# Moving the weight setup of a fused graph layer into the layer's own engine programs

## The reference

```python
x = x + gnn(layernorm(x), adj, wq, bq, wk, bk, wv, bv, wo, bo, w1, b1, w2, b2, alpha1, gamma1, alpha2, gamma2)
x = x + ffn(layernorm(x), gamma_in, slots1, gamma2, w_slot2, f_w1, f_b1, f_w2, f_b2)

def gnn(x, bias, ...):                      # 8 heads of 48 columns
    q, k, v = split_heads(x @ wq + bq), split_heads(x @ wk + bk), split_heads(x @ wv + bv)
    attn = softmax(q @ k.T * 48 ** -0.5 + bias)
    x = rmsnorm(x + (attn @ v) @ wo + bo, alpha1, gamma1)
    return rmsnorm(x + silu(x @ w1 + b1) @ w2 + b2, alpha2, gamma2)   # 384 -> 1536 -> 384
```

## Time and profile before

| | us |
|---|---|
| median of 3 runs | 3043.75 (3042.86 to 3047.78) |
| the profiled execution's own time | 3044.84 |
| its span in the profile | 3043.1 |
| mean granted TensorE clock | 0.979 of full |

### The profile page before, as it was taken

How to read it: one execution, slowest core, us unless ns; L and a number is a source line. 1 busy time by engine, 2 the same in 40 slices (tenths; PEclk the granted TensorE clock), 3 DMA queues, 4 the chain that set the end, 5 groups by cost and what they waited for, 6 DMA issues and landing times. The chain is left out here.

```text
span 3043.1 us, 63201 instructions
## 1 busy us (share of the span) xinstructions
PE 2847.6 (94%) x21971; PEld 2745.6 (90%) x21971; DVE 1898.3 (62%) x3029; ACT 1511.9 (50%) x3986; POOL 1476.6 (49%) x1486
## 2 busy tenths in 40 slices
PE   2899999999999999999999857999899999999996
PEld 2899999999999999999999846998899999999993
DVE  3466666666666666666666624765677777777764
ACT  3455454545555554545555424675455555544440
POOL 0344435354444434344444514553577777777760
PEclk9899999999999999999999968999999999999999
DMA  3010101011010101001010114552766666666799
GB/s 131 13 42 26 47 26 47 24 36 36 26 47 26 47 26 47 24 31 41 26 47 26 36 46 136 153 146 64 232 208 206 207 206 206 208 209 209 247 319 337
DMA packets 276739, 320.70 MB, mean 105 GB/s; under 512 B 17304, under 2 KB 275608, under 8 KB 276504
## 3 DMA queue, kind: packets, MB, share of 16 engines
q1 hardware_dynamic: 267960, 307.17, 32.4%
q10 hardware_dynamic: 8704, 12.58, 1.1%
HBM read 260.97 MB, written 58.72 MB: 105 GB/s over the span
## 5 line engine op out<-in xcount | busy, mean ns | idle before, releaser
L1567 PE MATMUL u_bank<-x_in,x_w 128*128 128x256 f32 x4608 | 574.1, 283 | 5.7 <-DVE x_w L1661 5.7
L1567 PEld LDWEIGHTS u_bank<-x_in,x_w 128*128 128x128 f32 x4608 | 569.2, 192 | 5.8 <-issue 5.8
L949 POOL TENSOR_TENSOR hT_lo<-h_tmp,hT_hi 128x512 fp32r<-128x512 f32 x192 | 247.1, 1287 | 454.0 <-DVE hT_hi L838 452.8
L1730 POOL TENSOR_TENSOR x_aT<-x_act,x_aT 128x512 fp32r<-128x512 f32 x128 | 299.4, 2339 | 181.2 <-ACT x_aT L1638 181.2
L411 PE MATMUL m_bank<-yT_hi,w_hi 128*128 128x256 f32 x1152 | 341.6, 296 | 1.5 <-ACT h_tmp L683 1.5
L1629 ACT ACTIVATE x_gelu<-u_bank,x_b1T 128x256 f32<-128x256 f32 x256 | 121.9, 476 | 408.6 <-PE u_bank L1567 408.6
L1726 POOL TENSOR_TENSOR x_w<-expert_raw,x_w 128x768 fp32r<-128x768 f32 x128 | 274.1, 2142 | 103.5 <-DVE x_w L1669 103.5
L411 PE MATMUL m_bank<-yT_hi,w_lo 128*128 128x256 f32 x1152 | 323.7, 281 | 0.0
L411 PE MATMUL m_bank<-yT_lo,w_hi 128*128 128x256 f32 x1152 | 323.5, 281 | 0.0
L683 ACT ACTIVATE h_tmp<-m_bank,b1c 128x256 f32<-128x256 f32 x384 | 157.2, 471 | 273.3 <-PE m_bank L411 273.0
L1579 PE MATMUL o_bank<-x_w,x_aT 128*128 128x384 f32 x1536 | 287.8, 335 | 1.8 <-POOL x_aT L1730 1.8
(11 more groups left out here) (216 smaller groups left out, 6936.4 us busy)
## 6 DMA issues: line engine op xcount, KB each, us to landing
expert_raw<-in_L_ffn_w_dram SPq DMA_DIRECT2D x384, 384.0 KB, 4.7
ws_raw<-in_L_ffn_w_slot_dram SPq DMA_DIRECT2D x32, 576.0 KB, 6.8
x_in<-in_x_dram SPq DMA_DIRECT2D x32, 384.0 KB, 3.3
x_res<-in_x_dram SPq DMA_DIRECT2D x32, 384.0 KB
residual<-f_sb SPq DMA_DIRECT2D x32, 384.0 KB, 2.5
yn<-yn_sb SPq DMA_DIRECT2D x32, 384.0 KB, 2.5
expert_out<-x_o SPq DMA_DIRECT2D x64, 192.0 KB, 3.0
slots2T<-residual SPq DMA_DIRECT2D x8, 1536.0 KB, 12.2
```

The source lines that it names most:

```text
L949: nc.gpsimd.tensor_tensor(hT[i % 3][1][:], h_tmp[i % 2][:], hT[i % 3][0][:].bitcast(F32), ALU.subtract).then_inc(hl.sem, 1)
L1567: mm = pe.matmul(u_bank[n % BANKS][:, g, :], w1s[i % 2][a][:, c, g, c2 * P:(c2 + 1) * P], xT[e % 2][b][:, c, :], start=c == 0 and j == 0, ...
L1730: nc.gpsimd.tensor_tensor(aTs[i % 2][1][:], aT[i % 2][:], aTs[i % 2][0][:].bitcast(F32), ALU.subtract).then_inc(al.sem, 1)
```

## The change

The setup block and its `free_semaphores()` go. What it did becomes part of the layer's programs, in the first two bodies, under `first(n)`, `first(a)` and `first(m)`, which are true for group 0 only; the loop's code is as before. The staging tiles now share SBUF with those layer tiles that are first written later (`s_sb`, `pT`, `yb`, `h_tmp`, `hT`, `f_sb`, `x_res` and others), so ACT waits for all of its hi copies before the first exponentials, and SP for w2's lo half before it loads `x_res`. The lo halves of w1 and w2, in three pieces each, are POOL's instead of DVE's. The 16 column DMAs of bq are issued by ACT.

```diff
@@ SP
                     sp.dma_start(x_in[:], x_rows[bass.ds(n * GN, GN), :].rearrange("(t p) d -> p t d", p=P)
                                  ).then_inc(x_landed.sem, 16)
+                    if first(n):
+                        for i in (WV, WQ, WK):
+                            load_weight(sp, i)
+                        sp.dma_start(rows["bv"][:], bv.partition_broadcast(P)).then_inc(bv_landed.sem, 16)
+                        sp.dma_start(phi[:], f_slots1.rearrange("k s d -> (k s) d")).then_inc(phi_landed.sem, 16)
+                        load_head_bias(sp, 1, bk)
...
                     sp.dma_start(adj_sb[:], adj[bass.ds(a * GT, GT)].rearrange("t q k -> q t k")
                                  ).then_inc(adj_landed.sem, 16)
+                    if first(a):
+                        load_weight(sp, WO)
+                        for name, src in (("bo", bo), ("alpha1", alpha1), ("gamma1", gamma1)):
+                            sp.dma_start(rows[name][:], src.partition_broadcast(P)).then_inc(rows_landed.sem, 16)
+                        load_weight(sp, W1)
+                        load_weight(sp, W2)
...
                 if m is not None:
+                    if first(m):
+                        sp.wait_ge(w_lo[W2].sem, len(w_copies[W2]))
@@ PE
+            def weight_ready(i):
+                pe.wait_ge(w_lo[i].sem, len(w_copies[i]))
...
+            def phi_transposed():
+                pe.wait_ge(phi_ok.sem, 4)
+                for c in range(DC):
+                    mm = pe.transpose(m_bank[0][:].rearrange("p a b -> p (a b)")[:, tok(c)], phi[:, tok(c)], ident[:])
+                mm.then_inc(phi_T.sem, 1)
...
                 if A: project(a, U_K, wk_s, 1)
+                if first(a): phi_transposed()
                 if M: down(m, 0)
                 if A: scores(a, 0, r); scores(a, 1, r)
@@ ACT
+            def weight_hi(i):
+                act.wait_ge(staged[i].sem, 16)
+                for src, hi, _ in w_copies[i]:
+                    nc.scalar.copy(hi, src).then_inc(w_hi[i].sem, 1)
...
+                if first(n): load_head_bias(act, 0, bq); weight_hi(WV)
+                if first(m): act.wait_ge(rest_landed.sem, 16 * N_REST)
                 if M: silu(m, 0)
                 if A: query(a, 0); query(a, 1)
...
+                if first(a): weight_hi(WO); weight_hi(W1); phi_transposed(); weight_hi(W2); act.wait_ge(consts.sem, 5)
                 if A: nc.scalar.activation(warm[:, 0:1], nhalf[:, 0:1], ACT.Exp)
                 if A: exps(a, 0, 0); exps(a, 0, 1); exps(a, 1, 0); prob_T(a, 0)
...
                 if N: hi_zT(n, 1)
+                if first(n): weight_hi(WQ); weight_hi(WK); phi_squares()
@@ DVE
+                if first(a): dve.wait_ge(bv_landed.sem, 16)
                 if A: values(a, 0); values(a, 1)
...
                 if A: key(a, 1)
+                if first(a): weight_lo(WO)
...
+                if first(n): head_masks()
                 if N: norm_stats(n, x_landed, 16, x_in, st, mv, stats, meanvar)
+                if first(n): weight_lo(WV)
                 if A: context(a, 0); recips(a, 1)
...
                 if N: lo_zT(n, 1)
+                if first(n): weight_lo(WQ); weight_lo(WK); head_biases(); phi_scaled()
...
+                if first(a): rows_scaled()
@@ POOL
+            def weight_lo(i):
+                for n, (src, hi, lo) in enumerate(w_copies[i]):
+                    pool.wait_ge(w_hi[i].sem, n + 1)
+                    nc.gpsimd.tensor_tensor(lo, src, hi.bitcast(F32), ALU.subtract).then_inc(w_lo[i].sem, 1)
...
+                if first(a): weight_lo(W1)
                 if N: power(n, 2, meanvar, mv[:, :, 1], eps_ln, rstd[:, 0, :], rstd[:, 1, :], ve, rstd_ok, 1)
+                if first(n): phi_power()
+                if first(a): weight_lo(W2); pool.wait_ge(rows_landed.sem, 16 * N_ROWS)
                 if M: h_lo(m, 2); h_lo(m, 3)
                 if A:
                     r_bias(a, 0)
```

More of the change, by code:

```diff
@@ L326, in setup_and_layer, with first, load_weight, load_head_bias @@
     S = lambda name, n: sem(ctx, name, n)
+    WQ, WK, WV, WO, W1, W2 = range(6)
+    weights, w_copies = (wq, wk, wv, wo, w1, w2), []
+    for i, parts in enumerate((wq_s, wk_s, wv_s, wo_s, w1_s, w2_s)):
+        if i < 2:
+            w_copies.append(by_head_parts(stage[i], parts))
+        elif i < 4:
+            w_copies.append([[t[:].rearrange("p c f -> p (c f)") if n else t[:] for n, t in enumerate((stage[i], *parts))]])
+        else:
+            views = [stage[i][:].rearrange("p (c f) -> p c f", c=(DC, FC)[i == W2]), *parts]
+            w_copies.append([[v[:, :, 512 * n:512 * n + 512] if i == W1 else v[:, 4 * n:4 * n + 4, :] for v in views]
+                             for n in range(3)])
+    staged, w_hi, w_lo = ([S(f"{name}{i}", 1) for i in range(6)] for name in ("staged", "w_hi", "w_lo"))
+    phi_landed, bv_landed, qk_landed, rows_landed, rest_landed = (S(n + "_landed", 16) for n in (
+        "phi", "bv", "bqk", "rows", "rest"))
+    N_QK, N_ROWS, N_REST = 4 * H, 3, 5 + FC
+    masks_ok, bias_ok, rows_ok = S("masks_ok", 6), S("bias_ok", 2), S("rows_ok", 2)
+    consts, phi_ok, phi_T = S("consts", 5), S("phi", 5), S("phi_T", 1)
+    def first(g):
+        return isinstance(g, int) and g == 0
+    def load_weight(eng, i):
+        w = weights[i]
+        eng.dma_start(stage[i][:].rearrange("p (c f) -> p c f", c=w.shape[0] // P), w.rearrange("(c p) f -> p c f", p=P)
+                      ).then_inc(staged[i].sem, 16)
+    def load_head_bias(eng, n, b):
+        column = b.rearrange("(h e o) -> h e o", e=DH, o=1)
+        for h in range(H):
+            m, g = divmod(h, 4)
+            eng.dma_start(bqk[HG * g:HG * g + HG, n, m:m + 1], column[h, 0:HG]).then_inc(qk_landed.sem, 16)
+            last = HG * g + (DH - HG) * m
+            eng.dma_start(bqk[last:last + DH - HG, n, 2:3], column[h, HG:DH]).then_inc(qk_landed.sem, 16)
     x_landed, adj_landed = S("x_landed", 16), S("adj_landed", 16)
@@ L428, in project @@
                     pe.wait_ge(held.sem, held.at(g, k))
+                if first(g) and n == 0:
+                    weight_ready(WQ if w is wq_s else WK)
                 bank = A_BANK[uses[n]]
@@ L440, in values @@
                         pe.wait_ge(yl.sem, yl.at(g - 1, 2))
+                    if first(g):
+                        weight_ready(WV)
                 bank = A_BANK[U_V[t]]
@@ L495, in project_out @@
                 pe.wait_ge(held.sem, held.at(g, k))
+                if first(g) and t == 0:
+                    weight_ready(WO)
                 bank = A_BANK[U_WO[t]]
@@ L512, in up @@
                 pe.wait_ge(yl.sem, yl.at(g, 2))
+                if first(g) and i == 0:
+                    weight_ready(W1)
+                    pe.wait_ge(phi_ok.sem, 5)
                 if i >= 2:
@@ L527, in down @@
                 pe.wait_ge(hl.sem, hl.at(g, i + 1))
+                if first(g) and i == 0:
+                    weight_ready(W2)
                 for t in range(GT):
@@ L634, in query @@
             def query(g, half):
+                if first(g) and half == 0:
+                    act.wait_ge(bias_ok.sem, 2)
                 act.wait_ge(a_full.sem, a_full.at(g, U_Q[half] + 1))
@@ L962, in body @@
                 if R: power(r, 2, mv2_ok, mv2[:, :, 1], eps_ln, rstd2[:, 0, :], rstd2[:, 1, :], ve2, rstd2_ok, 1)
+                if first(m): pool.wait_ge(rest_landed.sem, 16 * N_REST)
                 if M:
```

188 lines of the change are left out of this document (75 added, 113 removed).

## The result

The changed kernel takes **3014.57 us** (median of 4 runs, 3011.57 to 3015.6). The four runs of the kernel before have a median of 3044.45 us. The ratio is 0.9904, with a 95% interval of 0.9892 to 0.9917: 29.9 us faster at the median, where 34.0 were forecast. The profiled execution took 3015.42 us.

A forecast was written before the change was run, and what follows sets the result against it. PE is busy 94% of the span, so the gain must come from the start, where it works 0.87 of 48 us. -39.3 + 5.0 + 0.3 = -34.0 takes the median from 3043.75 to 3009.7 us, range 3003 to 3019.

The forecast's parts named there:

- part 3: Group 0's softmax: exponentials wait on ACT behind w2's load and copies, starting at 36.5; 5.0 us of the gain lost.
- The common mark: Start of group 1's values, 97.63 us before, 63.6 forecast; what it moves is the gain.
- My bound of 2 us for the time behind the mark: Group 1's values to the end: a difference over 2 us from before would make the whole forecast wrong.
- Part 1: Group 0's rows and wv at the start: z starts at 12.0 instead of 51.29, 39.3 us earlier.
- Part 2: wq, wk, biases and phi on DVE, phi's transposes and wo's subtract hide behind other work; costs nothing.
- Part 4: POOL's w1 and w2 subtracts, 3.5 us a piece, delay group 0's r_bias: 0.3 us lost, all slack used up.
- The clock: PE's clock, low after idling before the first probability transposes: could cost or gain 2 us; zero taken.
- A: Rival on the start: w2 lands earlier or its copies hide, all 39.3 us stay, 3004.4; 7%.
- B: Rival on SP's queue: bv, phi or bk issues stall, w1 and w2 land 7.8 us later, 3017.6; 13%.
- C: Rival on POOL: subtracts at the contended 6.5 us a piece delay r_bias, gain only 19.0, 3024.8; 12%.
- D: Rival on POOL's subtracts: pieces so slow, 9.7 us or beyond, that the gain is gone; slower kernel; 3%.

The follow-up runs named there:

- e2: Changed kernel with bq's 16 column DMAs issued by SP behind bk's instead of by ACT; 3016.13 us (one run).
- e1: Changed kernel with w2's hi copies and POOL's w2 subtracts moved behind group 0's attention; 3007.01 us, ratio to before 0.9874.
- e5: Changed kernel with the loads of rows bo, alpha1 and gamma1 issued behind w1 instead of ahead of it; 3015.05 us (one run).
- e3: Changed kernel with POOL forming the first piece of w2's lo half twice; 3015.92 us (one run).
- e4: Changed kernel with w2's lo half formed by DVE, ahead of the reciprocals, instead of POOL; 3013.43 us (one run).
- e8: Changed kernel with DVE's wait for the rows moved from right before group 0's y_scale to ahead of the reciprocals; 3018.86 us.
- e12: The changed kernel unaltered, run once more on the same chip; 3013.53 us (5 runs), ratio to before 0.9904.
- e7: Changed kernel with 12 larger bq/bk column DMAs, all on SP; wo, w1, w2 loaded before the second x_in; w2's halves after group 0's attention; 3008.88 us.
- e6: Changed kernel with wo, w1 and w2 issued right behind the bk columns, ahead of the second x_in; 3007.76 us, ratio to before 0.9878.
- e10: e7 with bq's columns back on ACT and group 0's adjacency loaded ahead of wo and w1; 3005.85 us, ratio to before 0.9873.
- e11: Changed kernel with 12 larger bq/bk column DMAs (six on ACT, six on SP) and w2's halves after group 0's attention; 3003.44 us, ratio to before 0.9867.

## Why the prediction was right, and where it was not

The prediction was right in sign and mechanism, and 3014.57 lies in the range of 3003 to 3019. It was 4.9 us too low: the start gained 0.7 less than forecast, the exponentials lost 4.5 more behind it (part 3), and the rest, with the stretch behind the mark, nearly cancels.

**The common mark** held: group 1's values moved by 28.7 and the span by 29.5. My bound of 2 us for the time behind the mark was met in that profile (0.8), but is too tight in general: the repeat of the same kernel was 5.1 below before.

**Part 1 (-39.3)**: -38.6. An ACT issue beside SP's cost 0.51 us (0.75 to 8.94 for 16), not 0.46. The nearest row was of the right columns, but of a single queue issuing; the first eleven issues took 0.53 each, the last five 0.47. Statistics, power, copy and subtract came as the rows said (1.02, 0.71, 1.15, 1.36).

**Part 2 (0)**: right. DVE was free of phi at 19.9 and PE met no wait for it; the scores and the wo subtract ended long before the exponentials. e2 shows that this stretch is cover: z 4.8 us earlier brought no gain.

**Part 3 (5.0 lost) is the step that was mis-sized: 9.5 were lost.** The mechanism is as put: ACT's order sets the exponentials behind w2's copies (41.66 and 41.67), and e1, which takes w2 out of that order, gives 7.5 us back. The size had two errors. First, w1: I took bytes at the rate of two 2304 KB loads. From the second `x_in` to w1's copy it took 16.0 us, not 12.9. In the window of 14 to 22 us, where adj, wo and the rows go, the DMA engines moved 224 GB/s at a share of 0.78. The kernel before, from 4 to 24 us, while large loads run:

```profile
4.00:24.00 20.00, 0.00 (x0) 0.00 (x0) 10.35 (x9) 11.39 (x10) 0.00 (x0) 1.00 1.05 388
```

388 GB/s at full share. e5 agrees in direction: 2.0 to 3.4 us for 576 KB of rows that by bytes take 1.4. The rate may not be all: over the 16.02 us the engines moved 302 GB/s, 4.8 MB, 0.8 MB more than the 3968 KB (4.06 MB) I counted, where before it was 0.3 MB more than 4608 KB. If the extra 0.5 MB are bytes of later loads that went in beside w1, they are an estimated 1.2 of the 3.1 us, by 388 GB/s; whose bytes they are I did not settle. Second, w2: its copy began 7.83 after w1's, where I had their landings 6.3 apart; ACT's own copies and phi end at 34.2, so all of it is waiting. With the 0.7 of part 1 that makes 0.7 + 3.1 + 1.5 = 5.3 of w2's delay against the forecast.

How much of this is the kernel and how much this one execution? In five profiles with this order of loads and w2 still ahead of the exponentials (the first, e3, e4, e8, e12) w2's copy began 21.3 to 23.9 us after the second `x_in` was issued, where I had 19.2. So at least 2.1 us were mis-sized in every one, and up to 2.5 more come and go by themselves; the first profile is the latest of the five.

**Part 4 (0.3 lost)**: right in mechanism, 0.1 in size. The pieces took 3.42 us against 3.5, from a line through two sizes; `r_bias` started 0.2 us after y was written, where it was 0.1 before. The estimate of 3.4 by the page GPSIMD Engine Reference of the Trainium skill (section Elementwise — side-by-side cycle accounting) agrees with 3.42. e3 shows that there was no slack, though in e12 there was (2.3 us, as y came late). Missed: half a us between `r_bias` and `y_scale`, which e4 and e8 lose again, for a cause not settled.

**The clock (0, ±2)**: 0 in the first profile (15.88 us from exponentials to `r_bias`, 15.99 before), 2.4 in e12 (18.35). The point value is one of two cases; the other lies just outside my bound. That the first profile met the value is luck, not my reasoning: I had PE idle for 7.7 us, and it idled for 13.2.

**Rivals.** A fell: ACT waited for w2. B fell here: SP's queue passed phi and bk without a stall (0.42 to 0.57 each) and stood still only behind w2, for 9.19 us, in front of rows that nobody wanted yet; e7 shows what it costs when somebody does. C fell here (3.42 a piece; wo's subtract, the only DVE instruction with two SBUF inputs near them, was over at 29.25, before POOL began at 31.16), but e5 (three pieces in 10.75), e6, e7 and e10 run into the contention. My reading that wo's subtract alone could meet POOL was too narrow: in e1, e3 and e11 POOL held up DVE instructions with one SBUF tile as input (last section). D was far off.

## What to carry to other kernels

When a prologue is merged into a software pipeline, the first group's start moves by nearly the whole prologue (38.6 us here), but what counts is the last thing that each in-order engine has queued ahead of the first group's own work. Put there only what that group needs: w2 belonged to a later stage, and moving it (e1) brought group 1's values 7.6 us forward. The best reordering of loads alone (e6) brought 6.7, and the times of the two don't differ clearly (3007.01 and 3007.76). On a queue, count issues and small loads by themselves, not by their bytes, and put nothing that is wanted soon behind two large loads.

## What the runs showed of the hardware

**Some DVE instructions and POOL's subtracts exclude each other for whole instructions, and not only where DVE reads two tiles.** e6: 4.61 us for a DVE subtract of 1.35 that met a POOL subtract. In e11 a DVE copy of 128x2 (L781), 0.17 us in the changed kernel, took 2.88 beside POOL's third piece; both ended together (38.03 and 38.01), and in e1 it took 2.89. POOL wasn't slowed by it. In e3 a DVE z of one graph (L786), 0.64 us in the changed kernel, took 3.19 beside POOL's extra piece:

```profile
55.78 3.19 DVE L786 TENSOR_SCALAR z<-x_in,mv,rstd 128x384 f32<-128x384 f32 x1
```

Others pass unhindered: beside POOL's pieces in e11 the sums with the adjacency, which read a PSUM and an SBUF tile, take 0.68 and the statistics of `x_in` 0.97, as they do without POOL. The page SBUF — State Buffer of the Trainium skill (section Who interferes with whom) has this rule: whichever starts first holds a shared pair of ports for its whole instruction, and copies in a two-port mode count as well as two SBUF inputs. The traces agree; that the copy or z was in such a mode no row shows. POOL's long instructions make it expensive: one of 3.4 us can delay a small DVE step of this kind by up to that much.

**The first issue behind w1 and w2, 2304 KB each, takes 6.8 to 9.6 us** (9.19 in the changed kernel, 6.79 in e6, 7.03 in e7, 9.58 in the earlier trace rows), whatever it loads: a row, `x_in` or phi. Behind w1 alone, in e5, it takes 0.49.

Open: the half us in front of `y_scale`, 3.07 in most profiles and 2.6 in two; why adj, wo and the rows flowed at little more than half the rate of the large loads, why w2's landing varies by up to 2.5 us, and what varies by up to 8 us (2940.4 to 2948.8) over the long shared stretch.
